# Products of the bf16 identity with itself, ahead of waits of TensorE in an eight-stage transformer kernel

## The reference

```python
x = _layernorm(x + _L0_attn_ref(x, ...))   # 16 heads of 8, causal softmax
x = _layernorm(x + _L0_ffn_ref(x, ...))    # two layers of local attention, window 64, and a gated MLP
x = _layernorm(x + _L1_attn_ref(x, ...))   # 16 heads of 8, relative positions (shifted)
x = _layernorm(x + _L1_ffn_ref(x, ...))    # 8 experts, the best 2
x = _layernorm(x + _L2_attn_ref(x, ...))   # 16 heads of 8, ALiBi, causal
x = _layernorm(x + _L2_ffn_ref(x, ...))    # ternary MLP, 128-512-512-512-128
x = _layernorm(x + _L3_attn_ref(x, ...))   # 16 heads of 64, clipped relative positions
x = _layernorm(x + _L3_ffn_ref(x, ...))    # 16 experts in groups, the best 4, and a shared one
```

## Time and profile before

| | us |
|---|---|
| median of 3 runs | 2304.55 (2299.51 to 2312.35) |
| the profiled execution | 2308.97 |
| its span, first to last instruction | 2307.3 |
| mean granted TensorE clock | 0.955 |

### The profile page before, as it was taken

The page is one execution under the profiler, slowest core; times in us unless marked ns, Lnnn a source line. Parts: engine busy times, 40 slices in busy tenths (PEclk is TensorE's granted clock), DMA queues, the critical chain, the costliest instruction groups (busy, mean ns, idle before and its releaser), DMA issues.

```text
span 2307.3 us, 40672 instructions
## 1 busy us (share of the span) xinstructions
PE 2030.2 (88%) x15704; PEld 1226.8 (53%) x15704; DVE 1536.3 (67%) x3079; ACT 1136.8 (49%) x1854; POOL 746.6 (32%) x1057
## 2 busy tenths in 40 slices
PE   5886789988868989998998898998999999999888
PEld 2342466666644455445564344445666666666546
DVE  5685678888678777755556774024877777777663
ACT  2575456656614454563332566223664655646442
POOL 4544434333037847441002331002223232232133
PEclk7998899999979999999998999999999999999999
DMA  4430111111323524202002320001664564645252
GB/s 139 127 100 2 29 29 29 33 24 29 97 86 118 152 67 141 70 16 102 1 1 64 106 71 2 31 1 56 182 184 147 157 184 132 185 148 157 80 112 55
DMA packets 183975, 198.87 MB, mean 86 GB/s; under 512 B 55922, under 2 KB 152486, under 8 KB 179302
## 3 DMA queue, kind: packets, MB, share of 16 engines
q1 hardware_dynamic: 183782, 196.27, 28.9%
HBM read 93.53 MB, written 92.08 MB: 80 GB/s over the span
## 4 chain that ended last, share of the span: by engine, by line
PE 34%; DVE 10%; ACT 4%; DMA 3%; issue 2%; SPq 1%; POOL 1%; DVEq 0%; ACTq 0%; POOLq 0%
PE PS L2097 5%; DVE AR L2411 4%; PE PS L1950 3%; PE PS L2326 3%; PE PS L2333 2%; PE PS L1937 2%; PE PS L1940 2%; DMA RA<-ZP 2%; PE PS L2295 2%; PE PS L2348 2%; PE PS L2675 1%; ACT AR L2491 1%; DVE PS L2408 1%; PE PS L597 1%; PE PS L2365 1%
## 5 line engine op out<-in xcount | busy, mean ns | idle before, releaser
L2491 ACT ACTIVATE AR<-PS,AR 128x512 f32<-128x512 f32 x256 | 173.6, 686 | 181.1 <-DVE AR L2411 181.0
L1275 ACT ACTIVATE AR<-PS 128x1024 f32<-128x1024 f32 x160 | 162.6, 1024 | 124.4 <-PE PS L1024 123.5
L2537 POOL TENSOR_TENSOR RA<-AR,RA 128x288 f32<-128x288 f32 x128 | 88.0, 698 | 374.6 <-ACT AR L2491 190.1
L718 ACT ACTIVATE AR<-PS 128x1024 f32<-128x1024 f32 x160 | 162.8, 1024 | 94.1 <-PE PS L576 46.4
L1128 DVE TENSOR_REDUCE AR<-PS 128x2 f32<-128x768 f32 (+1 forms) x192 | 159.9, 864 | 56.1 <-PE PS L1004 29.5
L2411 DVE TENSOR_REDUCE AR<-PS 128x2 f32<-128x1024 f32 x128 | 156.7, 1224 | 9.0 <-DVE PS L2408 0.5
L2333 PE MATMUL PS<-CC,AR 128*128 128x128 f32 x1024 | 140.0, 280 | 20.1 <-DVE AR L2417 16.0
L2333 PEld LDWEIGHTS PS<-CC,AR 128*128 128x128 f32 x1024 | 110.3, 141 | 72.3 <-issue 37.7
L2326 PE MATMUL PS<-AR 64*128 64x200 f32 (+2 forms) x1280 | 131.4, 349 | 3.0 <-ACT AR L2491 3.0
L1821 POOL TENSOR_TENSOR AR<-AR 128x1024 f32<-128x1024 f32 x32 | 75.5, 2358 | 174.9 <-DVE AR L1669 174.9
L2326 PEld LDWEIGHTS PS<-AR 64*128 64x128 f32 x1280 | 103.8, 188 | 39.4 <-issue 29.8
(11 more groups left out here) (367 smaller groups left out, 4978.2 us busy)
## 6 DMA issues: line engine op xcount, KB each, us to landing
ZD<-RC SPq DMA_DIRECT2D x32, 1152.0 KB
AR<-ZD SPq DMA_DIRECT2D x32, 640.0 KB
ZP<-AR SPq DMA_DIRECT2D x128, 160.0 KB, 2.6
SP<-AR SPq DMA_DIRECT2D x40, 384.0 KB, 2.6
AR<-SP SPq DMA_DIRECT2D x128, 96.0 KB
RA<-SP SPq DMA_DIRECT2D x32, 384.0 KB
SP<-AR SPq DMA_DIRECT2D x40, 256.0 KB, 2.9
RC<-RC SPq DMA_DIRECT2D x64, 130.0 KB
```

The lines of the kernel that those rows point to most:

```text
L718: e.activation(self.PT[m % 6], C.PS[:, 2 * s:2 * s + 2, :], ACT.Exp).then_inc(S["s_turned"].sem, 1)
L1275: e.activation(self.PT[m % 6], C.PS[:, 2 * s:2 * s + 2, :], ACT.Exp).then_inc(S["s_turned"].sem, 1)
L2491: i = e.activation(self.PP[n % 5][:, hh, 16:528], C.bank[2 * (n % 2) + hh], ACT.Exp, bias=self.NMX[n % 4][:, hh:hh + 1], accum_out=self.DE ...
L2537: e.tensor_tensor(self.XM[:, 2 * q:2 * q + 2, :], self.PP[n % 5][:, :, 128 * q:128 * q + 144], W["edge"].unsqueeze(1).broadcast_to((128, 2 ...
```

## The change

`fill` issues n products of the bf16 identity `idb` (128 x 128) with itself, broadcast four times to 512 columns, into a bank. `start=True` and `stop=True` make each overwrite the bank; the product of the step behind overwrites it again. Tables `FILLED` give n by step. In `scores` and `turned` the wait for the free bank moves ahead of the wait for the data, and the fill stands between. In `Local` there are two new steps of the plan, `("fill", 27)` and `("fill", 31)`, ahead of `("scores", 27)` and `("scores", 31)`; each takes a bank of the ring and frees it by a signal of TensorE's own, and its last product is 128 columns wide.

```diff
+def fill(e, C, o, n):
+    one = C.W["idb"]
+    for _ in range(n):
+        e.matmul(o.rearrange("p (c j) -> p c j", c=4), one, one.unsqueeze(1).broadcast_to((128, 4, 128)), start=True, stop=True)
...
 class Paired:
+    FILLED = {0: {("scores", 0): 40, ("turned", 10): 11, ("turned", 25): 4, ("turned", 70): 5, ("turnx", 2): 8, ("turnx", 3): 12},
+              2: {("turned", 0): 10, ("turnx", 2): 6, ("turnx", 3): 6}}
...
+        filled = self.FILLED[self.kind].get(step, 0)
...
             s = self.slots.slot[step]
+            w.wait_ge(*self.slots.freed(*step))
+            fill(e, C, C.bank[2 * s], filled)
             w.wait_ge(S["y_rows", k % 2], k)
-            w.wait_ge(*self.slots.freed(*step))
...
         elif kind == "turnx":
             b, = key
+            fill(e, C, b7, filled)
             w.wait_ge(S["v_fin"], b)
...
 class Shifted:
+    FILLED = {("turned", 40): 11, ("turned", 80): 5}
...
 class Local:
+    FILLED = {("lin", 0, 0): 11, ("v", 0): 11, ("turnq", 0): 20, ("turnq", 8): 8, ("fill", 27): 10, ("fill", 31): 14, ("ot", 30): 8,
+              ("turnx", 2): 6, ("two", 7): 16, ("four", 7): 9}
...
+            if n in (27, 31):
+                plan.append(("fill", n))
...
             o = self.bank(step)
+            if step == ("v", 0):
+                fill(e, C, C.bank[0], self.FILLED[step])
             w.wait_ge(S["s_square"], 3, 1)
             w.wait_ge(*self.ring.freed(*step))
+        if kind == "fill":
+            fill(e, C, o, self.FILLED[step] - 1)
+            e.matmul(o[:, 0:128], W["idb"], W["idb"], start=True, stop=True).then_inc(S["t_fill"].sem, 1)
+        elif step in self.FILLED and kind != "v":
+            fill(e, C, o, self.FILLED[step])
...
 class Experts, turnx:
+            if b == NB - 1:
+                fill(e, C, C.bank[7], 13)
             w.wait_ge(S["v_fin"], b)
...
 class Clipped, rel:
+            if u == 0:
+                fill(e, C, o, 7)
             w.wait_ge(S["s_table"])
...
 class Clipped, turnx:
+            if b == NB - 1:
+                fill(e, C, o, 12)
             w.wait_ge(S["v_fin"], b)
```

More of the change, by code:

```diff
@@ L1016, in on_tensor @@
             s = self.slots.slot[step]
+            w.wait_ge(*self.slots.freed(*step))
+            fill(e, C, C.bank[2 * s], self.FILLED.get(step, 0))
             w.wait_ge(S["y_rows", k % 2], k)
             w.wait_ge(S["v_init"], 3)
-            w.wait_ge(*self.slots.freed(*step))
             for r in range(2):
@@ L1430, in __init__ @@
         self.parts = {
-            "t": {"lin": 1, "v": 1, "turnq": 1, "turnk": 1, "scores": 1, "flip": 1, "av": 1, "ot": 1, "out": 1, "two": 1, "hg": 1, "ha": 1, "four": 1, "five": 1, "turnx": 1},
+            "t": {"lin": 1, "v": 1, "turnq": 1, "turnk": 1, "scores": 1, "flip": 1, "av": 1, "ot": 1, "out": 1, "two": 1, "hg": 1, "ha": 1, "four": 1, "five": 1, "turnx": 1, "fill": 1},
             "v": {"init": 1, "lin": 1, "sum": 1, "norm": 3, "turnk": 1, "soft": 2, "av": 2, "out": 1, "ln": 5, "two": 1, "ha": 1,
@@ L1450, in __init__ @@
                                          "flip": S["s_flip"], "ot": S["s_ot"], "out": S["v_out"],
-                                         "two": S["v_two"], "hg": S["s_hg"], "ha": S["v_ha"], "four": S["v_four"], "five": S["s_five"],
+                                         "fill": S["t_fill"], "two": S["v_two"], "hg": S["s_hg"], "ha": S["v_ha"], "four": S["v_four"], "five": S["s_five"],
                                          "turnx": S["s_turnx"]}, lambda step: many.get(step, range(6)))
```

## The result

| | before | after |
|---|---|---|
| median, us (range) | 2306.01 (2299.51 to 2312.35), 6 runs | 2291.47 (2287.44 to 2294.61), 6 runs |
| the profiled execution, us | 2308.97 | 2291.35 |
| its span, us | 2307.3 | 2289.6 |
| mean granted clock in the profile | 0.955 | 0.973 |

The account below looks back on a forecast made before the run. TensorE, busy 88%, was taken as the main engine, slowed by 208 us at the lower clock after waits; gains 10.8 + 7.5 + 1.9 + 4 = 24.2, three quarters kept (18), from 2304.55 gave 2286.5 us, range 2267 to 2305.

Parts of the forecast that it names:

- four places where the clock was to read 1.00: Sign: full granted clock behind `turned` 10, `turned` 25, `turnq` 0 and `turnx` 3 of `Clipped`.
- No site but one makes its successor late; what hides the products is the same wait.: All 24 sites: products fit the existing waits, except `turned` 0 of the second Paired stage, costing up to 2.2 us.
- The start of `Local`, 7.5 us.: `lin` 0, `turnx` 3 with `v` 0, `turnq` 0: VectorE waits for TensorE throughout; 7.5 us gained.
- Ten mid stretches, 10.8 us.: Ten lower-clock stretches of about 3.4 us in the first Paired stage, `Local` and `Shifted`: 1.08 us each, 10.8 gained.
- The end of `Local`, 4 us.: `turnx` 2, `two` 7, `four` 7 beside the head of `Shifted`: a third of some 14 us on the path; 4 gained.
- `turnx` 3 of `Clipped`, 1.9 us.: Product pairs of L2663 and L2665 behind this site on the chain run at full clock: 1.9 us gained.
- The two Paired starts, 0.: Starts of both Paired stages: TensorE's lower-clock time nearly free beside VectorE; second start's gains offset by ten products; 0.
- Three quarters of the sum are kept.: Of the 24.2 us summed over the sites, 18 are kept, since idle remainders of 1 to 2 us lose some.
- the clock isn't held: Rival at the filled sites: clock falls within the products, which outlast their waits; 2315 us, at worst 2332; chance 0.10.
- TensorE is the bound nearly everywhere: Rival behind the sites: half of 96.4 us goes, less what remainders lose; 2268 us; chance 0.09.
- Absorbed: Rival in Paired, Shifted and Local: clock held, but DMA round trips and VectorE absorb the time; 2300.5 us; chance 0.23.

Follow-up runs that it names:

- experiments 5 and 6: Changed kernel without its wide products, moved waits and ring steps kept: 2307.4 us; kernel before with only the three moved bank waits: 2307.53 us.
- experiment 1: Changed kernel with all 261 wide products cut from 512 columns to 16: 2300.27 us, ratio 0.9969 to the kernel before.
- kernel 8: Changed kernel with counts trimmed where products outlast the wait, and nine products added at `scores` 55 of both Paired stages: 2290.7 us, ratio 0.9934.
- experiment 2: Changed kernel without the four fillings at the start of `Local` (`lin` 0, `v` 0, `turnq` 0, first-stage `turnx` 3): 2297.67 us, ratio 0.9964.
- experiment 10: Changed kernel without the forty products of `scores` 0 of the first stage: 2293.35 us, ratio 0.9954.
- experiments 1 and 11: Changed kernel with 16-column products everywhere: 2300.27 us; with 16-column products outside `Local` and none in it, ring steps keeping their 128-column product: 2301.19 us.

## Why the prediction was right, and where not

The time (2291.5 against 2286.5) and the sign came out, and the main reasoning held: mean clock 0.973 where I had written about 0.975; products 0.216 us apart; no time from the moved waits and ring steps (experiments 5 and 6); the clock held by the work of the products (experiment 1). The range held too. That the number came so near is in part luck, as the last step below tells. Of the four places where the clock was to read 1.00 three do; `turnq` 0 doesn't.

The Trainium skill ("TensorE: Matmul & The Clock Gate", Back-to-back issue gap) gives 131 ns for a sustained stream of this shape. The trace disagrees: the fillings that run wholly at the full clock stand 0.216 to 0.219 us apart, which is the figure that the Trainium skill gives for a product alone.

Step by step:

- *"No site but one makes its successor late; what hides the products is the same wait."* This failed. I read each wait as one for data. At `turnq` 8, `turned` 40 and 80 and the extra `scores` 55 of kernel 8 part of the wait or all of it is for the bank. `scores` 0 and `v` 0 are the first products behind the opening of a stage, where TensorE waits until every engine has done its last step of the stage before (`opening` in `program`), a third kind of wait beside those for data and for a bank; the filling stands behind that wait and can't use it. At ten of 24 sites the successor starts right at the end of the filling. `v` 0 is the clearest. Before, it waited 3.65 us for ScalarE and started 4.28 us behind the turn of `turnx` 3 (230.98 against 226.70). Now TensorE idles 2.95 us at the opening, until ScalarE's copy of the last turned block is done; then the eleven products take 4.22 us, partly at the lower clock, and `v` 0 starts 7.66 us after the turn (230.91 against 223.25), 3.4 us late. Half of that shows in the period, 17.59 against 15.88 us; from `turnx` 2 to `turnq` 0 the filled kernels with no or three products there take 47.3 to 47.6 us, those with eleven 48.3 to 49.1. TensorE before, then ScalarE's copy in the changed kernel:

```profile
230.98 5.28 PE L1558 MATMUL PS<-RA,AR 128*128 128x512 f32 x8 [3.65 <-ACT AR L1765]
...
226.16 0.59 ACT L749 ACTIVATE XT<-PS 128x512 f32<-128x512 f32 x1
```

- *The start of `Local`, 7.5 us.* The traces show none of it on the way to `turnq` 0: 21.19 against 21.12 us in its first part, 1.7 lost in the second. Behind `turnq` 0 I expected a clock of 1.00 and 3 us less. It is 0.61 and 0.9 less: the filling ends 2.01 us before the data, and the clock falls in what remains. Yet leaving these fillings out costs 6.2 us (experiment 2). In its trace the way to `turnq` 0 is 1.5 us shorter than in the changed kernel and the next part, to `turnq` 8, 2.1 longer (86.8 against 84.7), so most of the 6.2 isn't found near the start. That gap isn't closed; part may be places of packets rather than these products, which wasn't tested.
- *Ten mid stretches, 10.8 us.* Right in kind, but not by site. `Shifted` gave 6 to 8 where two sites at 1.1 were in the sum. `turned` 40 to 50 went from 23.1 to 21.6 us and 80 to 90 from 22.8 to 21.6, about as priced, though the 16-column products have the first of the two as well. But 130 to 140, which isn't filled, went from 22.5 with 6.8 us at the lower clock to 20.3 with none. I had left unfilled stretches as they were, and they aren't.
- *The end of `Local`, 4 us.* 6.9 on the way to `four` 7 less 2.3 on the way to `two` 6: 4.6.
- *`turnx` 3 of `Clipped`, 1.9 us.* From the turn to the product of L2646 8.65 us (2207.71 less 2199.06), now 7.06 (2189.43 less 2182.37): 1.6.
- *The two Paired starts, 0.* For `scores` 0 experiment 10 doesn't contradict it (2 to 4 us, within the uncertainty). In the second, the real product of `turned` 0 starts 16.85 us behind the turn against 15.85, a microsecond lost as foreseen, and the first period behind it runs at 1.00 and takes 8.06 us. Leaving out both starts costs 6 us by the medians and 3.5 by the ratios. By the parts, kernels that fill the second start alike take 44.7 to 47.9 us to `turned` 15 and those without 45.1 to 47.7, so I can't say where it lies.
- *Three quarters of the sum are kept.* What was kept is 14.5 of 24.2, six tenths. That it came so near rests on two things that I didn't have, of opposite sign: products that outlast their waits take back (`v` 0 above), and about 6 us came with the added instructions and not with the clock (experiments 1 and 11).

Of the rivals, *the clock isn't held* falls with 0.973; *TensorE is the bound nearly everywhere* asked for 36 us. *Absorbed* has its share: 84 us less at the lower clock bought 14.5, 0.17 us each. Between experiment 1 and the changed kernel lie 0.973 - 0.956 of clock, 78 us, and 8.8 us of time: 0.11 each, where one on TensorE's path would have bought half a microsecond.

## What to carry to other kernels

Filler on TensorE is worth having where a wait drops the clock and the work behind it is on the path, but only the part of the wait that begins once a bank is free, and once every wait ahead of the step is over, can be filled, and each product beyond it is delay; so read from the trace which of the two waits ends last, and start with half of what would fit, which here brought as much as all of it. Judge it by several timed runs and a control with the same instructions and no work in them: such a control, with hardly any work in it, moved this kernel by 0.2 to 0.3%. And clock that is won back is worth a fraction of its half where other engines or DMA round trips set the pace.

## What the runs showed of the hardware

- The queue "instruction" moves data beside the kernel's own DMAs. In one round trip a packet of 16,384 bytes took 0.95 us there, and packets of a small write came right behind it: 4.17 us instead of 2.22. The Trainium skill ("Runtime: NRT & Kernel Launch", Instruction fetch mechanics) says that an engine's sequencer fetches its instructions in blocks of 16 KiB over a DMA queue of its own, and calls the cost mostly hidden. The size agrees with the trace. Whether the fetch is hidden from the engine no run here tells; from the DMAs beside it, at this place, it wasn't.
- The same 261 instructions leave the mean clock at 0.956 with hardly any work in them (0.955 without them), and bring it to 0.973 with 512 columns each.
- The clock can fall behind short waits too. In the changed kernel it fell 0.3 us after the wait of 2.01 us at `turnq` 0, and 1.5 us after the one of 1.54 ahead of 1236.35, with another of 0.73 between. Behind 1.26 us at `Clipped` and 2.75 us at `turned` 10 it stayed up.
